# A hand-ordered attention loop with its transposes gathered in one run per tile, and two PSUM places moved

## What is computed

```python
enc, ca = encoder_hidden_states[:, :150, :], encoder_hidden_states[:, 150:, :]
hs = _mha(hidden_states @ Wq, enc @ Wk, enc @ Wv)
ca_q1 = jnp.einsum('btc,th->bch', ca, Wq_ca)[:, indices, :]
ca_hs1 = _mha(ca_q1, residual, residual)
ca_hs2 = _mha(ca_hs1 @ Wq, ca @ Wk_ca, ca @ Wv_ca)
out = (hs + ca_hs2) @ Wout + b_out + residual
```

## Time and profile before

| | us |
|---|---|
| median of 3 runs | 1575.46 |
| lowest, highest | 1571.61, 1577.05 |
| the profiled execution, in all | 1574.71 |
| its span, first to last instruction | 1572.9 |
| PE busy | 1520.7 (97%) |
| PEld busy | 1245.3 (79%) |
| DVE busy | 792.3 (50%) |
| ACT busy | 621.4 (40%) |
| mean granted TensorE clock | 0.993 |

### The profile page before, as it was taken

How to read it: one execution, slowest core, us unless ns; L and a number is a source line. 1 busy time by engine, 2 the same in 40 slices (tenths; PEclk the granted TensorE clock), 3 DMA queues, 4 the chain that set the end, 5 groups by cost and what they waited for, 6 DMA issues and landing times.

```text
span 1572.9 us, 24610 instructions
## 1 busy us (share of the span) xinstructions
PE 1520.7 (97%) x10294; PEld 1245.3 (79%) x10294; DVE 792.3 (50%) x1595; ACT 621.4 (40%) x1310; POOL 2.8 (0%) x12
## 2 busy tenths in 40 slices
PE   6999999999999999999999999999999999999999
PEld 4763589999975378998997438989898744898998
DVE  5686335344468453543447816335345772443533
ACT  1427724233243852332333583233233267333322
POOL 0000000000000000000000000000000000000000
PEclk9999999999999999999999999999999999999999
DMA  6530012130253001122035200113004410021101
GB/s 237 200 132 35 2 43 76 48 120 25 84 175 123 1 6 56 64 79 83 27 109 186 85 1 20 61 49 150 18 34 160 168 36 1 19 93 56 60 18 43
DMA packets 46680, 117.27 MB, mean 75 GB/s; under 512 B 3661, under 2 KB 5317, under 8 KB 45019
## 3 DMA queue, kind: packets, MB, share of 16 engines
q1 hardware_dynamic: 37036, 93.91, 17.1%
q10 hardware_dynamic: 9535, 21.80, 3.6%
HBM read 77.33 MB, written 39.17 MB: 74 GB/s over the span
## 4 chain that ended last, share of the span: by engine, by line
PE 83%; DVE 7%; ACT 7%; issue 3%; DMA 0%; SPq 0%; ACTq 0%
PE ps_w L500 41%; PE ps_s L500 17%; PE ps_t L500 15%; PE ps_t L510 9%; DVE unit_max L1283 4%; ACT work L1100 4%; ACT work L1070 1%; DVE ot L1449 1%; ACT ot L1132 1%; PE ps_s L510 1%; ACT ot L1015 0%; DMA y_all<-in_L_xattn_Wv_ca_dram 0%; PE ps_w L510 0%; DVE xt_l L1368 0%; DVE neg_max L1337 0%
## 5 line engine op out<-in xcount | busy, mean ns | idle before, releaser
L500 PE MATMUL ps_w<-wo_h,ot 128*128 128x320 f32 x1280 | 327.2, 321 | 0.2 <-DVE ot L1449 0.2
L1283 DVE TENSOR_REDUCE unit_max<-ps_s 128x1 f32<-128x512 f32 x384 | 240.1, 684 | 51.3 <-PE ps_s L500 49.8
L500 PEld LDWEIGHTS ps_w<-wo_h,ot 128*128 128x128 f32 x1280 | 222.7, 189 | 0.6 <-DVE ot L1449 0.5
L500 PE MATMUL ps_w<-wo_l,ot 128*128 128x320 f32 x640 | 197.9, 309 | 0.0
L1070 ACT ACTIVATE work<-ps_s,neg_max 128x150 f32<-128x150 f32 x512 | 161.0, 399 | 41.3 <-DVE neg_max L1341 41.3
L500 PE MATMUL ps_w<-v_all,work 120*128 120x162 f32 (+1 forms) x1280 | 171.3, 289 | 0.0
L500 PEld LDWEIGHTS ps_w<-v_all,work 120*128 120x128 f32 x1280 | 169.1, 191 | 0.8
L1061 ACT ACTIVATE work<-ps_t 120x512 f32<-120x512 f32 (+1 forms) x128 | 62.9, 491 | 225.7 <-PE ps_t L510 225.7
L510 PE MATMUL ps_t<-ident,work 128*120 128x128 f32 (+1 forms) x960 | 140.0, 276 | 2.0 <-ACT work L1061 1.0
L500 PE MATMUL ps_s<-keys_h,qt_h 128*128 128x300 f32 (+1 forms) x448 | 134.9, 301 | 0.6
L1337 DVE TENSOR_REDUCE neg_max<-ps_s 128x6 f32<-128x900 f32 x64 | 70.1, 1096 | 126.4 <-PE ps_s L500 126.4
(11 more groups left out here) (160 smaller groups left out, 2217.1 us busy)
## 6 DMA issues: line engine op xcount, KB each, us to landing
xc<-in_x_dram SPq DMA_DIRECT2D x32, 1280.0 KB, 6.5
out_dram<-work ACTq DMA_DIRECT2D x64, 320.0 KB, 2.2
xt_all<-work SPq DMA_DIRECT2D x60, 256.0 KB, 2.2
xt_l<-xt_all SPq DMA_DIRECT2D x12, 1280.0 KB, 5.6
y_all<-in_L_xattn_Wk_dram SPq DMA_DIRECT2D x4, 960.0 KB
y_all<-in_L_xattn_Wv_dram SPq DMA_DIRECT2D x4, 960.0 KB
pick<-pick_all SPq DMA_DIRECT2D x16, 194.0 KB
xc<-in_L_xattn_Wq_dram SPq DMA_DIRECT2D x1, 1600.0 KB, 10.6
```

Of the source, the lines that this page charges most:

```text
L500: return nc.tensor.matmul(out, lhs, rhs, start=start, stop=stop, skip_group_check=True)
L1283: v.tensor_reduce(unit_max[:, a, n, q:q + 1], bank, AX_X, ALU.max).then_inc(max_free, 1)
```

## The change

It is in the main loop and in what feeds it.

- `turn_weights` turns all ten pieces at once at the start of a slot. The last two go to bank 0 of `ps_w` (`t2_bank`), with semaphores of their own (`t2_full`, `t2_free`), instead of a `ps_t` bank.
- `turn_o` writes to `ot_psum`, which is bank 1 of `ps_w` and the first 128 columns of bank 2, instead of both banks of `ps_t`. It waits for `ya_ready` now.
- The value products are in banks 0 and 2, the projection's halves in banks 1 and 0. Half 1 waits for `on_first`, which DVE sets when the first half of the tile is normalised.
- From slot 2 to 13 the order is: ten weight transposes, [queries], scores of s+1, [gather], values, projection of s-1 whole, `turn_o`. In slots 14 and 15 `turn_o` stands within half 1 after three fifths of it.
- ACT and DVE follow: ACT takes the remaining weights right after the first ones; the turned output is taken at the end of a slot, or, where the next slot holds queries, in that slot ahead of them. DVE's sum of half 1 stands ahead of the low part, except in slots 14 and 15.
- Outside the loop, a turned statistics tile goes to bank 1 instead of 0 of `ps_w`, and the turned `ca` rows to `ps_t` instead of `ps_w`.

The diff, cut to its core:

```diff
-        z_banks = [ps_s[0:WIN, 0, :], ps_w[0:WIN, 0, :]]
+        z_banks = [ps_s[0:WIN, 0, :], ps_w[0:WIN, 1, :]]
+        t2_bank = ps_w[0:KR, 0, 0:(VT - 2 * GRP) * P]
+        o_banks = [ps_w[:, 0, 0:GRP * VW], ps_w[:, 2, 0:GRP * VW]]
+        ot_psum = ps_w_flat[:, CHUNK:CHUNK + HID]
+        out_banks = [ps_w[:, 1, 0:HALF], ps_w[:, 0, 0:HALF]]
...
-                    last = turned(ps_w[:, 2, c * TOK:(c + 1) * TOK], ca_rows4[:, c * P:(c + 1) * P])
+                    last = turned(ps_t[:, 1, c * TOK:(c + 1) * TOK], ca_rows4[:, c * P:(c + 1) * P])
...
                 def queries(c):
-                    pe.wait_ge(ot_low, tile0 + c * ST - 1)
...
-                def turn_weights(s, parts):
-
-                    if parts[0] == 0:
-                        if s:
-                            pe.wait_ge(ot_low, tile0 + s)
-                        pe.wait_ge(p_ready, tile0 + s + 1)
-                    for part in parts:
+                def turn_weights(s):
+
+                    pe.wait_ge(p_ready, tile0 + s + 1)
+                    for part in range(2):
...
+                    if s > 1:
+                        pe.wait_ge(y_ready, START + tile0 + s - 1)
+                    for n in range(2 * GRP, VT):
+                        q = n - 2 * GRP
+                        last = turned(t2_bank[:, q * P:(q + 1) * P], probs[:, KR * n:KR * (n + 1)])
+                    last.then_inc(t2_full, 1)
 
                 def values(s):
-                    banks = (2, 0)
+
+                    pe.wait_ge(t2_free, tile0 + s + 1)
...
-                        if n == VT_HALF:
-                            pe.wait_ge(ya_ready, START + tile0 + s)
...
+                        if n == VT_HALF and s:
+                            pe.wait_ge(ot_low, tile0 + s)
...
                 def turn_o(s):
+
                     pe.wait_ge(on_ready, tile0 + s + 1)
-                    for bank in range(2):
-                        pe.wait_ge(t_free[bank], before(b, ("o", s, bank)))
+                    if s:
+                        pe.wait_ge(ya_ready, START + tile0 + s)
+                    else:
+                        pe.wait_ge(z_done, PHASES * (b + 1))
                     for j in range(KT):
-                        last = turned(ps_t_flat[:, j * P:(j + 1) * P], o_norm[:, j * P:(j + 1) * P])
+                        last = turned(ot_psum[:, j * P:(j + 1) * P], o_norm[:, j * P:(j + 1) * P])
...
                 for s in range(SLOTS):
                     c, t = divmod(s, ST)
-                    if s and s + 1 < SLOTS:
-                        if t == ST - 1:
-                            queries(c + 1)
-                        if s > 1:
-                            tile_scores(s + 1)
-                    turn_weights(s, (0, 1))
+                    ahead = c + 1 < CHUNKS
+                    turn_weights(s)
+                    if ahead and t == ST - 1:
+                        queries(c + 1)
                     if s == 1:
+                        project(0, 0, range(0, 3))
                         gather(0)
-                    if s:
+                        project(0, 0, range(3, KT))
+                    elif 1 < s < SLOTS - 1:
+                        tile_scores(s + 1)
+                    elif s:
                         project(s - 1, 0)
-                    turn_weights(s, (2,))
-                    if c + 1 < CHUNKS and t == GATHER_AT:
+                    if ahead and t == GATHER_AT:
                         gather(c + 1)
                     values(s)
                     if s == 0:
                         tile_scores(2, (0,))
                         turn_o(0)
                         tile_scores(2, (1, 2))
-                    if s:
-                        project(s - 1, 1, range(0, 2))
-                    if s:
+                    elif s < SLOTS - 2:
+                        if s > 1:
+                            project(s - 1, 0)
+                        project(s - 1, 1)
                         turn_o(s)
-                    if s:
-                        project(s - 1, 1, range(2, KT))
+                    else:
+                        if s < SLOTS - 1:
+                            project(s - 1, 0)
+                        project(s - 1, 1, range(0, 3))
+                        turn_o(s)
+                        project(s - 1, 1, range(3, KT))
```

More of the change, by code:

```diff
@@ L76, in turns @@
         ahead = c + 1 < CHUNKS
-        if t == ST - 1 and ahead:
-            order += [("q", c + 1, j) for j in range(KT)]
-        order += [("p", s, part) for part in range(2)]
+        order += [("p", s, 0), ("p", s, 1)]
         if s == 1:
             order.append(("gather", 0))
[L82 to L86, removed]
+        if ahead and t == ST - 1:
+            order += [("q", c + 1, j) for j in range(KT)]
+        if ahead and t == GATHER_AT:
+            order.append(("gather", c + 1))
     used, copied, use, bank = [0, 0], [0, 0], {}, 1
     for name in order:
-        bank = name[2] if name[0] == "o" else 1 - bank
+        bank = 1 - bank
         use[name] = (bank, used[bank], copied[bank])
         used[bank] += 1
-        copied[bank] += name[0] != "o"
+        copied[bank] += 1
     return use, used, copied
@@ L834, in turn_weights @@
                         pe.wait_ge(t_free[bank], before(b, use))
-                        for n in range(GRP * part, min(GRP * (part + 1), VT)):
+                        for n in range(GRP * part, GRP * (part + 1)):
                             q = n - GRP * part
@@ L877, in project @@
                         rows = slice(kt * P, (kt + 1) * P)
-                        mm3(ps_w[:, half, 0:HALF], ot_h[:, s % 2, rows], ot_l[:, s % 2, rows], wo_h[:, kt, cols],
+                        mm3(out_banks[half], ot_h[:, s % 2, rows], ot_l[:, s % 2, rows], wo_h[:, kt, cols],
                             wo_l[:, kt, cols], kt == 0, False)
@@ L1063, in remaining_weights @@
                 def remaining_weights(s):
-                    use = ("p", s, 2)
-                    turned_weights(probs_t[0:KR, 2 * GRP:VT, :],
-                                   ps_t[0:KR, bank_of(use), 0:(VT - 2 * GRP) * P].rearrange("p (r s) -> p r s", s=P), use)
+                    act.wait_ge(t2_full, tile0 + s + 1)
+                    nc.scalar.activation(probs_t[0:KR, 2 * GRP:VT, :], t2_bank.rearrange("p (r s) -> p r s", s=P),
+                                         copy).then_inc(t2_free, 1)
                 def weight(s, h):
@@ L1124, in _ @@
                         nc.scalar.activation(p2[:, :, :], s2[:, :, :], exp, scale=SCALE).then_inc(e2_ready, 1)
+                        take_output(0)
                     if s > 1:
                         store(s - 2)
-                    if s and c + 1 < CHUNKS:
+                    if c + 1 < CHUNKS:
                         for kt in X_AT[t]:
                             x_high(c + 1, kt)
-                    for bank in range(2):
-                        act.wait_ge(t_full[bank], filled(b, ("o", s, bank)))
-                    nc.scalar.activation(ot_h[:, s % 2, :], ps_t_flat[:, 0:HID], copy).then_inc(ot_high, 1)
-                    if s == 0:
-                        for kt in X_AT[0]:
-                            x_high(1, kt)
+                    if s and not queries_next(s + 1):
+                        take_output(s)
                 if b + 1 < B:
@@ L1392, in normalise, with output_low @@
                                                o_rec[:, r * GRP:(r + 1) * GRP].unsqueeze(2).broadcast_to([P, GRP, DH]), ALU.mult)
[L1393 removed]
+                        last.then_inc((on_first, on_ready)[r], 1)
+                def output_low(s):
+                    dve.wait_ge(ot_high, tile0 + s + 1)
+                    v.tensor_tensor(ot_l[:, s % 2, :], ot_psum, ot_h[:, s % 2, :], ALU.subtract).then_inc(ot_low, 1)
                 def add_rows(s, half):
```

81 lines of the change are left out of this document (36 added, 45 removed).

## The result

The changed kernel takes 1563.63 us (median of 4 runs, 1562.20 to 1564.23) against 1575.57 us of the kernel before on the same chip: a ratio of 0.9928, 95% interval 0.9915 to 0.9941. The forecast was 1565.4 in a range of 1560 to 1572. The profiled execution took 1563.7 us with a span of 1561.6, 11.3 less than before.

What follows compares the result with a forecast made beforehand. TensorE, busy 97% of the span, bounds the kernel, so only gaps between matmul starts can be saved. Terms 5.6 + 0.1 + 2.3 + 1.3 + 0.6 - 0.35 = 9.5, taken as 9.3: 1574.7 - 9.3 = 1565.4 us, range 1560 to 1572.

Steps and rivals of the forecast that it cites:

- T5's wait: Turned output's five transposes, slots 1 to 14: waiting for DVE's normalisation ends, 0.10 us a slot, 5.6 us in all.
- The queries: Head of query matmuls, slots 3, 7, 11: shorter wait, now for ACT's copy; 0.19 us each, 2.3 us in all.
- Slots 0 and 1: Start of each batch: last two weight transposes run ahead in idle time; 0.32 us a batch, 1.3 us in all.
- Slot 15: Last weight transposes stall 0.3 us for DVE's sum instead of 0.46; gain 0.15 a batch, 0.6 us in all.
- A: Rival: the turned output's 0.10 us is the cost of turning to transposes, still paid; 1571.1 us, chance 0.15.
- B: Rival: turned output's transposes held by DVE's sum behind two x_low; 1591 us if 2 us late, chance 0.04.
- C: Rival: each run of 15 transposes in the main loop brings the clock to half; 1660 us, chance 0.03.
- D: Rival: faster than forecast, queries without stall and slots 0 and 1 better by 0.9 us; 1560.5 us, chance 0.08.

Runs made afterwards that it cites:

- late_output: Kernel before the change, with only the turned output's five transposes moved behind the whole of projection half 1, in the old banks; 1592.55 us, 1.0112 of before.
- three_groups: Changed kernel with its run of 15 transposes broken into three groups between score matmuls, in slots with scores and no queries; 1564.30 us, 0.9928 of before.
- both_waits: Changed kernel with slot 1's x_low behind the gathered rows' copy, and four projection matmuls held back to stand ahead of the queries; 1558.76 us, 0.9905 of before.
- x_low_later: Changed kernel with DVE's two x_low subtractions in slot 1 moved behind the copy of the gathered rows; 1563.50 us, 0.9931 of before.

## Why the prediction was right

**The place.** Only gaps between starts could be won. Most of them do not show as idle time: TensorE was counted busy for 225.3 of 227.06 us in a loop before and for 223.5 of 224.4 after, so of the 2.7 us the counted idle time gave 0.9, and 1.8 came out of counted busy time of the same matmuls.

**T5's wait** (5.6 us in the sum): the step proved to be a wait for DVE's normalisation, by late_output, three_groups and slot 14. Slots fell from 11.75 to 11.64; twelve intervals a batch won 0.11. The two around slots 1 and 14, where a half projection changes its place, won 0.28 together, of which 0.15 is slot 15's term; 4 x (12 x 0.11 + 0.13) = 5.8.

**The queries** (2.3): the three slots of a batch that hold queries fell by 0.34, 0.32 and 0.31, 0.11 of each being T5's; the rest is 0.21 a slot or 2.6 us, against 0.19 forecast. The wait that takes its place is the one named, ACT's copy: it is 0.30 us from the last transpose to the first query matmul (the row of two transposes starts 0.41 ahead) and 0.34 to the second. The timeline, against the earlier trace rows:

```profile
213.00 0.38 PE L512 MATMUL ps_w<-ident,work 128*120 128x128 f32 x2
213.41 0.50 PE L502 MATMUL ps_t<-xt_h,wq_h 128*128 128x512 f32 x1
213.75 0.40 PE L502 MATMUL ps_t<-xt_l,wq_h 128*128 128x512 f32 x1
```

**Slots 0 and 1** (1.3): value products 0 and 1 are 10.68 us apart, were 11.09. From that 0.41 goes a new wait: the values of slot 0 start 1.73 us after the first transpose (182.37 to 184.10) instead of 1.56 (183.98 to 185.54), as they now want ACT's last copy at once, since it frees their own bank. What is left is 0.24 a batch, 1.0 us. This is slot 1's 0.22 and hardly more: the 0.10 that the forecast gave to slot 0 did not come. It had that the two transposes no longer wait for ACT's first copy, but not that the values would wait for ACT's second. The stall in slot 1 stayed, as forecast, and two rows show how DVE still ends it, against the earlier trace rows:

```profile
193.60 0.31 PE L502 MATMUL ps_w<-wo_h,ot 128*128 128x320 f32 x1
194.53 0.41 PE L502 MATMUL ps_w<-vw_b,p_rows 98*128 98x320 f32 x1 [0.62 <-DVE p_rows L1383]
```

**Slot 15** (0.6, and 0.35 lost at the end): the last two transposes wait for DVE's sum, 0.3 us, where 0.46 was lost before; the tail is 0.4 us longer.

```profile
404.69 1.04 PE L512 MATMUL ps_t<-ident,work 128*120 128x128 f32 x8
405.88 0.43 PE L512 MATMUL ps_w<-ident,work 128*120 128x128 f32 x2
```

Eight transposes usually take 0.87 to the start of the ninth; here it comes at 1.19.

Together 5.8 + 2.6 + 1.0 + 0.6 - 0.4 = 9.6, where 9.3 was forecast. The windows agree: 10.7 in the loops, less 0.7 for the wait ahead of the first values of each and 0.4 in the tail. That the terms sum so closely is in part luck: T5 and the queries came out 0.2 and 0.3 better, slots 0 and 1 0.3 worse. The total fell by more than the sum, 11.9 us by the medians; the clock falls, which the forecast did not count either way, are the part that differs.

**The rivals.** A (the 0.10 is the price of switching) fell with late_output and three_groups: at most 0.01 us a slot. B (T5 behind DVE's sum) did not occur: the margin was worked out as 0.7 us; in the profile after, DVE's sum of slot 4 ends 0.77 ahead of T5.

```profile
251.07 0.48 DVE L1416 TENSOR_TENSOR work<-ps_w,xc 128x320 f32<-128x320 f32 x1
```

(One reading in this working was off, without effect: the 0.42 us from a projection's last matmul to DVE's sum were DVE's own queue, whose low part ended at 255.71; where DVE is free, it is 0.35, from 252.17 to 252.52.) With 1.06 us more on the sum, in one run, the kernel is slightly slower than before (1577.38 against 1574.68), so the rival was a real one: about 1 us later and the gain is gone, where the forecast had 1.2. Its price a slot was right; its count of slots (20) left out slots 1, 14 and 15. C (clock) did not occur even with a run of 43. D (queries without stall) did not happen by the change, but both_waits shows that it can be had.

## What to carry to other kernels

When an engine's matmuls are back to back, what a reordering can win is the sum of the gaps between starts, and these can be read from the starts in the timeline to a few hundredths of a us, while the busy share stays at 97%; ask of each gap which engine ends just ahead of it. Moving work to get cover costs the waits of whatever now stands behind it: here late transposes of the output were worth 0.11 us a slot, but only with banks that the queries do not need. Where slots repeat to a few hundredths of a us and the total wanders by several, judge a small edit by its slots, not by its median, and look at the granted clock of each execution.

## What was not expected of the hardware

A fall of the clock to half for 3.4 us costs 1.1 to 1.7 us of a stretch between loops, and its places differ between executions of one program: the changed kernel had them at 123.9, 482.3 and 881.6 us in its first profile, and in its second none between loops (154.2, 154.2 and 154.5 us) but one more in the first stretch (at 41.0 and 122.9, 185.2 us instead of 184.1). That is as much as any single term of this change but the first two. And an edit that took 2.9 us out of the loops (x_low_later) left the median where it was, at a lower clock. What brings a fall about is not shown.
